# Transposing the probabilities one step sooner in a fused decoder layer: half 0 ahead of the scores, half 1 behind them

## The reference

```
x = layernorm(x + attn(x))      # linear attention: state = prod_k (K_k^T V_k), per head of 16, then out projection
x = layernorm(x + xattn(x))     # cross attention on 64 context rows, 16 heads of 64:
                                #   sim = q k^T / 8;  p = softmax(sim) over 64 keys;  out = p v, then Wout, + b_out
x = layernorm(x + ffn(x))       # 8 experts, 256 -> 1024 -> 256, each token weighted by its routing softmax
```

## Time and profile before

| | us |
|---|---|
| median of 3 runs | 1261.03 |
| the profiled execution | 1261.79 |
| its span | 1260.1 |
| TensorE matmuls busy | 1219.2 |
| TensorE weight loads busy (beside the matmuls) | 1100.2 |
| VectorE busy | 868.0 |
| ScalarE busy | 567.2 |
| GpSimd busy | 623.7 |

### The profile page before, as it was taken

The page is one execution under the profiler, slowest core; times in us unless marked ns, Lnnn a source line. Parts: engine busy times, 40 slices in busy tenths (PEclk is TensorE's granted clock), DMA queues, the critical chain, the costliest instruction groups (busy, mean ns, idle before and its releaser), DMA issues.

```text
span 1260.1 us, 24107 instructions
## 1 busy us (share of the span) xinstructions
PE 1219.2 (97%) x8848; PEld 1100.2 (87%) x8848; DVE 868.0 (69%) x1694; ACT 567.2 (45%) x1117; POOL 623.7 (50%) x986
## 2 busy tenths in 40 slices
PE   8979999999999999999999999988999999999998
PEld 7868889898898898988988989887798899899888
DVE  5557888888888888888888888887533323322435
ACT  2144556555546465556465655555423312421420
POOL 3245766766756767567567575665322112202201
PEclk9999999999999999999999999999999999999999
DMA  9820111102111111111111211220221021022001
GB/s 275 222 74 19 43 35 51 51 26 60 39 39 44 35 51 52 31 56 43 35 49 29 58 45 31 84 81 26 69 92 57 12 67 68 1 68 68 1 1 35
DMA packets 117912, 69.88 MB, mean 55 GB/s; under 512 B 74658, under 2 KB 115363, under 8 KB 117796
## 3 DMA queue, kind: packets, MB, share of 16 engines
q1 hardware_dynamic: 115764, 67.67, 18.3%
q10 hardware_dynamic: 2032, 0.66, 0.2%
HBM read 42.09 MB, written 26.22 MB: 54 GB/s over the span
## 4 chain that ended last, share of the span: by engine, by line
PE 79%; DVE 9%; issue 2%; POOL 1%; ACT 1%; POOLq 0%; DVEq 0%
PE ob L137 7%; PE ob L138 6%; PE ob L139 6%; PE sim L137 6%; PE sim L138 6%; PE sim L139 6%; PE pw L440 4%; PE pw L137 3%; PE pw L138 3%; PE pw L139 3%; PE pt L489 3%; PE pw L390 3%; PE pt L139 2%; PE pt L138 2%; PE pt L137 2%; DVE prob L848 2%
## 5 line engine op out<-in xcount | busy, mean ns | idle before, releaser
L1595 POOL TENSOR_TENSOR w_lo<-w_raw,w_hi 128x2048 fp32r<-128x2048 f32 x16 | 73.7, 4609 | 222.5 <-ACT w_hi L1535 169.3
L137 PE MATMUL ob<-b_hi,pT_hi 128*128 128x256 f32 x512 | 153.3, 299 | 14.6 <-DVE pT_lo L855 14.6
L138 PE MATMUL ob<-b_lo,pT_hi 128*128 128x256 f32 x512 | 144.5, 282 | 0.0
L139 PE MATMUL ob<-b_hi,pT_lo 128*128 128x256 f32 x512 | 144.2, 282 | 0.0
L950 POOL TENSOR_TENSOR prob<-prob,rz 128x512 f32<-128x512 f32 x128 | 130.9, 1044 | 10.4 <-DVE rz L796 10.4
L711 ACT ACTIVATE prob<-prob 128x512 f32<-128x512 f32 x128 | 80.8, 631 | 112.0 <-DVE prob L848 111.4
L843 DVE TENSOR_REDUCE mx<-sim 128x8 f32<-128x512 f32 x128 | 88.2, 689 | 40.1 <-PE sim L139 39.1
L137 PEld LDWEIGHTS ob<-b_hi,pT_hi 128*128 128x128 f32 x512 | 97.5, 190 | 19.4 <-DVE pT_lo L855 18.7
L137 PE MATMUL sim<-a_hi,tT_hi 128*128 128x512 f32 x256 | 103.9, 406 | 0.0
L623 ACT ACTIVATE x<-h,nmr,rstd 128x256 f32<-128x256 f32 x128 | 76.3, 596 | 58.5 <-POOL nmr L869 53.7
L138 PE MATMUL sim<-a_lo,tT_hi 128*128 128x512 f32 x256 | 101.3, 396 | 0.0
(11 more groups left out here) (245 smaller groups left out, 3839.1 us busy)
## 6 DMA issues: line engine op xcount, KB each, us to landing
xraw<-in_x SPq DMA_DIRECT2D x16, 512.0 KB, 3.8
kv_scratch<-stage SPq DMA_DIRECT2D x32, 256.0 KB, 3.1
x_scratch<-x SPq DMA_DIRECT2D x64, 128.0 KB, 1.7
out_x<-o_sb SPq DMA_DIRECT2D x64, 128.0 KB, 1.7
w_raw<-in_L_ffn_experts_inter SPq DMA_DIRECT2D x8, 1024.0 KB, 5.1
w_raw<-in_L_ffn_experts_out SPq DMA_DIRECT2D x8, 1024.0 KB, 7.6
kraw<-kv_scratch SPq DMA_DIRECT2D x32, 128.0 KB, 2.9
vraw<-kv_scratch SPq DMA_DIRECT2D x32, 128.0 KB, 2.9
```

Source lines behind the costliest of these rows:

```text
L137: pe.matmul(out, lh, rh, start=first, stop=False)
L138: pe.matmul(out, lh, rl, start=False, stop=False)
L139: return pe.matmul(out, ll, rh, start=False, stop=last)
```

## The change

In each slot that has a tile n - 1, half 0 of the transposes moves ahead of the scores on TensorE, to just behind the first preparations (and ahead of the norm of x1) on ScalarE, and to just ahead of the first maximum on VectorE. Half 1 takes half 0's old place on all three. Nothing else changes; the lists of GpSimd and of the DMA queue are the same.

```
@@ pe_slot
+        if has_prev:
+            pe_pT(pe, n - 1, (slot - 1) % 2, 0)
         if has_sim:
             pe_sim(pe, it, slot, 0)
         prep(1)
...
         prep(2)
         if has_prev:
-            pe_pT(pe, n - 1, (slot - 1) % 2, 0)
+            pe_pT(pe, n - 1, (slot - 1) % 2, 1)
         prep(3)
...
         prep(5)
-        if has_prev:
-            pe_pT(pe, n - 1, (slot - 1) % 2, 1)
         prep(6)
@@ act_slot
         prep(0)
+        if has_prev:
+            act_pT(act, n - 1, 0)
         if has_x1T:
...
         prep(3)
         if has_prev:
-            act_pT(act, n - 1, 0)
+            act_pT(act, n - 1, 1)
         if has_sim:
             act_exp(act, n, q, 1)
...
-        if has_prev:
-            act_pT(act, n - 1, 1)
         prep(8)
@@ dve_slot
             dve_stats(dve, 2, n - 2, q, h2[:, q, :])
+        if has_prev:
+            dve_pT(dve, n - 1, 0)
         if has_sim:
             dve_max(dve, n, 0)
...
         prep(5)
         if has_prev:
-            dve_pT(dve, n - 1, 0)
+            dve_pT(dve, n - 1, 1)
         if has_sim:
             need(dve, "exp_made", 2 * n + 2)
...
-        if has_prev:
-            dve_pT(dve, n - 1, 1)
         if (it, slot) == (NB - 1, 0):
```

## The result

The changed kernel takes 1287.62 us (median of 6 runs, 1287.15 to 1288.05), the kernel before, run beside it, 1261.14 us (6 runs, 1260.58 to 1262.26). The ratio is 1.0208, with a 95% interval of 1.0197 to 1.0218: slower by 26.5 us. The profiled run took 1287.15 us with a span of 1285.4 us, 25.3 more than the span before; TensorE's granted clock was 0.997 in both.

What follows compares the result with a forecast made beforehand. It took TensorE as the bound, with VectorE close behind in three slots. Rounds 14 x (2.28 + 0.34 - 0.28) = 32.8, ends +1.0 - 5.0 + 0.7, sum +29.5: 1290.5 us, range 1281 to 1299.

Steps and rivals of the forecast that it cites:

- The old wait: TensorE's wait for pT_lo in slot 2 of every round, listed at 0.77 us, priced at 1.03, would go.
- one on prob: In slot 2 the transposes would wait on p_ready; the slot takes 9.58 instead of 9.86, -0.28 us per round.
- Slot 3, ScalarE's list: pT_hi stands behind the waiting a_hi of A1, and pT_lo ahead of VectorE's maximum: +2.28 us per round.
- The bounds of slot 3: From below +0.44 us, the later scores alone; from above +3.1, everything from the old maximum on moved.
- Rival (B): Only the 0.44 us shift acts, ScalarE's block in slot 3 being caught up: 1265 us, chance 0.09.
- Slot 1: b_lo of the second context product comes later and T1's weight load waits for its bank: +0.34 us per round.
- Slot 0: VectorE's 1.69 us idle before the maximum covers the 0.44 us shift: costed at nothing, 0.44 at most.
- The ends: Slot 3 of round 14 +1.0 us, remaining waits in the last two rounds -5.0, the last slot of all +0.7.
- the waits left over: Waits after 788.10, in the last two rounds, worth 10 us, of which about half comes back: -5.0.
- Those named as signs: New TensorE waits for prob, a_lo, zw_lo and b_lo, and VectorE's pT_lo waiting some 1.8 us in slot 3.
- The price of a step on VectorE: 0.60 us by the rows; by the DRAIN page 0.08 longer per extra step, 2.4 us more, an estimate.

Runs made afterwards that it cites:

- experiment 2: The changed kernel with the new order only in slots 0, 1 and 2, slot 3 in the old order: 1250.48 us, ratio 0.9914.
- experiment 3: The changed kernel with the new order in slot 2 alone, all other slots in the old order: 1245.93 us, ratio 0.9884.
- experiment 4: The changed kernel with GpSimd normalising half 0 of prob ahead of the inverse deviation of z in all slots: 1275.82 us, ratio 1.0115.
- experiment 1: The changed kernel with ScalarE copying half 0 (pT_hi) ahead of A1's copy in slot 3: 1263.51 us, ratio 1.0016.
- experiment 6: The changed kernel with VectorE making B2's b_lo ahead of z's statistics in slot 1: 1284.83 us, ratio 1.0180.
- experiment 9: The changed kernel with ScalarE's copy of half 0 in slot 3 two copies later, behind A0's copy: 1304.97 us, ratio 1.0344.
- experiment 5: The changed kernel with the new order only in slot 2 of every round and slots 0 and 3 of the last round: 1244.59 us, ratio 0.9858.

## Why the prediction was right, and where its sizes were off

It said 1290.5 us in 1281 to 1299, slower; 1287.62 is inside, and the waits stand in the trace where it put them. By its own steps:

- **The old wait goes, and one on prob takes its place in slot 2.** Predicted 9.58, measured 9.57 to 9.59. Experiments 2 to 4 show each half: without the successor the slot is 8.86 to 8.92, so the old wait was worth 1.00 (I had 1.03 from the matmuls' starts, where its row lists 0.77).
- **Slot 3, ScalarE's list.** Predicted +2.28, measured +1.88; mechanism right, a term of the sum mis-sized. Up to pT_lo and the maximum the steps hold: S + 4.09 and S + 4.70 against 4.05 and 4.65. Then three small ones. The a_lo of A1 starts 0.60 behind the maximum, not 0.72, at S + 5.30: the 0.72 is met elsewhere only, behind a maximum whose next step is the shift. From this a_lo to the last one the list takes 7.13 us, not the 7.35 of before, since VectorE no longer stands for zw_hi (0.10 from mv to zw_lo; before, half 1's pT_hi was ahead of zw_hi on ScalarE, and it was 0.21) and loses a few hundredths in other steps. And Q0 to the end of the slot takes 4.31, not 4.39. Together 0.09 + 0.22 + 0.08 = 0.39. "No gap, so moves by the same 2.27" was the failing inference: the steps of a list without gaps still had 0.2 us in them.
- **The bounds of slot 3.** The lower one, +0.44 if ScalarE held nothing up, was built as experiment 1: +0.28. Rival (B), 1265, was near that kernel's 1263.51 and not near this one.
- **Slot 1.** Predicted +0.34, measured +0.28, and experiment 6 ties it to T1's wait for b_lo.
- **Slot 0.** Predicted nothing, measured 0.02 less. Round: 52.6 predicted, 52.11 measured.
- **The ends.** Predicted -3.3, measured -0.6 in two parts. Not foreseen: in the first batch slot 1 starts with a wait of 1.31 us for prob, and the slot behind it comes 1.1 later. In the last two rounds I had +1.0 - 5.0 + 0.7 = -3.3, and the slots gave -1.7: the slot 3 of round 14 +0.83, the last slot +0.63, both close; but of the waits left over, worth 5.0 in my sum, only 3.1 came back. The last round's slots 0, 2 and 3 gained 1.70, 0.68 and 0.58, while its slot 1 gained 0.02, as it hangs on x2T_lo of the feed-forward part (2.8 us in the waits above, 1.8 before), and in slot 1 of round 14 b_lo ends the wait that pT_lo ended before (1.28 us at 852.46 in place of 1.32).
- **The waits.** Those named as signs came, some at other sizes: the transposes for prob 0.51 (named: 0.6), A2 for a_lo 0.80 (1.1), SW for zw_lo 0.25 (0.5), and on the rows of the weight loads Q0 for a_lo 0.46 (0.3) and T1 for b_lo 0.24 (0.2). VectorE waited 2.33 us for pT_hi (1.8).
- **The price of a step on VectorE.** Where the steps were moved, pT_lo starts at 453.94 with 0.69, the maximum at 454.55, the a_lo at 455.15, 0.61 and 0.60 apart; each starts before the listed end of the one before. The Trainium skill, page "VectorE: DVE Perf Modes", section "The DRAIN you can't avoid", has the next operation start only when the pipe is empty, but adds that one that is not held starts earlier. The prediction gave only the first half of this; the trace agrees with the second, and the 2.4 us that I had priced by the first did not come.

In the sum: 26.0 (rounds) + 1.1 (first batch) - 1.7 (last rounds) = 25.4, and the feed-forward part starts at 926.07 instead of 900.69, 25.4 later. Predicted were 32.8 and -3.3; the 6.8 us too much in the rounds were partly offset by the 2.7 too little at the ends. That was luck, and so was 1.1 us more: the medians are 26.5 us apart, the feed-forward starts of the two profiled runs 25.4. By the rounds alone the forecast was a quarter too high, 2.34 us a round against 1.86.

## What to carry to other kernels

A step that is moved ahead is only sooner if the list it enters is not waiting there: look, on each engine, at what stands just ahead of its new place and when that one is released. The dangerous spot is a step for other work that waits (here A1's copy, 3.4 us idle), since everything on the next engine's list then waits with it. Decide such an order per slot and not for all slots alike: the same move gave 1.0 us in slot 2 and cost 1.9 in slot 3. Two fixes that each pay alone (24 and 12 us here) need not add, when the second was paid with a wait that the first removes.

## What the runs showed of the hardware that I had not expected

A wait of under 2 us can be followed by a lower clock. Behind A2's wait of 1.77 us in experiment 9 the granted clock fell to 0.50, the level of 1.2 GHz, in three rounds of fourteen, at 0.69 us each, while the same wait left the other eleven slots at 18.45 to 18.47. In the changed kernel, where that wait is 0.80 us, no slot 3 of the 14 rounds is longer than 17.50. The kernel before has one such fall too, in slot 1 of the last round, behind waits of 1.77 us for x2T_lo and 0.54 for pT_lo. Experiment 3 has the same instructions in this slot, with the same two waits, and no fall. Slot 1 of the last round, before and in experiment 3, columns as in the earlier trace rows:

```profile
859.72:873.37 13.65, 11.12 (x70) 9.92 (x69) 10.68 (x19) 6.67 (x13) 8.05 (x7) 0.88 0.06 20
845.08:857.52 12.44, 9.91 (x70) 8.71 (x69) 10.68 (x19) 6.68 (x13) 8.05 (x7) 1.00 0.07 22
```

The fall costs 13.65 - 12.44 = 1.21 us. It came in this slot in the profiled runs before and after the change, so it cancels between them; of the ten experiments only 3 and 4 were profiled without it. Differences of about 1 us between two kernels, as between experiments 3 and 5, can't be read without looking at this slot.

And TensorE's listed idle time is less than what a wait costs: rows of 0.77 us were worth 1.00 us in the time of the slot. The row of the weight load in front of the same matmul comes closer:

```profile
436.33 0.19 PEld L137 LDWEIGHTS ob<-b_hi,pT_hi 128*128 128x128 f32 x1 [0.97 <-DVE pT_lo L855]
```
